# Routing inside the tile loops, weights by expert, and masks turned by the DMA: one change to a two-layer graph and expert network

## The reference, cut to what matters

```python
x = x + gnn0(layernorm(x), adj)    # attention over the neighbours: softmax of h @ h.T where adj > 0
x = x + ffn0(layernorm(x))         # 8 experts, top 2 of each node, hidden 512, silu(x@w1) * (x@w3) @ w2
x = x + gnn1(layernorm(x), adj)    # relu((adj @ x) @ W.T + b)
x = x + ffn1(layernorm(x))         # 8 experts, top 2 of each node, hidden 1024, gelu(x@w1.T + b1) @ w2.T + b2
```

## Time and profile before

| what | us |
|---|---|
| three timed runs | 1803.61, 1805.94, 1807.93 (median 1805.94) |
| the profiled execution, its own time | 1815.38 |
| its span, first to last instruction | 1813.4 |
| mean granted TensorE clock, share of 2.4 GHz | 0.938 |

### The profile page before, as it was taken

How to read it: one execution, slowest core, us unless ns; L and a number is a source line. 1 busy time by engine, 2 the same in 40 slices (tenths; PEclk the granted TensorE clock), 3 DMA queues, 4 the chain that set the end, 5 groups by cost and what they waited for, 6 DMA issues and landing times. The chain is left out here.

```text
span 1813.4 us, 36020 instructions
## 1 busy us (share of the span) xinstructions
PE 1560.3 (86%) x9584; PEld 1297.9 (72%) x9584; DVE 1149.1 (63%) x3860; ACT 638.9 (35%) x1349; POOL 698.7 (39%) x1336
## 2 busy tenths in 40 slices
PE   5899999999999934999999559989618999999994
PEld 5788888888888823888888426555307888888894
DVE  5457777777777766556655356666685666666652
ACT  2323333333333311322233152222205565555562
POOL 0122232233222112767767304333404555455551
PEclk9899999999999966999999869999859999999997
DMA  6233434433333344333323434555341222222223
GB/s 108 86 120 132 149 139 148 149 131 130 130 130 139 102 160 148 53 50 48 50 49 52 101 106 157 195 195 194 110 191 31 41 35 38 38 35 35 38 37 93
DMA packets 85362, 184.70 MB, mean 102 GB/s; under 512 B 19789, under 2 KB 62539, under 8 KB 81291
## 3 DMA queue, kind: packets, MB, share of 16 engines
q1 hardware_dynamic: 57386, 128.02, 21.4%
q0 software_dynamic: 22656, 31.07, 10.8%
q10 hardware_dynamic: 5280, 25.17, 3.5%
HBM read 132.66 MB, written 54.99 MB: 103 GB/s over the span
## 5 line engine op out<-in xcount | busy, mean ns | idle before, releaser
L1056 PE MATMUL bank<-ffn_w_in_parts,ffn_x_t 128*128 128x512 f32 x1416 | 361.7, 404 | 1.7 <-DVE ffn_w_in_parts L1195 1.6
L1080 PE MATMUL bank<-ffn_w_out_parts,ffn_hidden_t 128*128 128x256 f32 x2124 | 285.2, 288 | 19.6 <-DVE ffn_hidden_t L1185 19.6
L1056 PEld LDWEIGHTS bank<-ffn_w_in_parts,ffn_x_t 128*128 128x128 f32 x1416 | 259.4, 191 | 56.0 <-DVE ffn_w_in_parts L1195 5.1
L1080 PEld LDWEIGHTS bank<-ffn_w_out_parts,ffn_hidden_t 128*128 128x128 f32 x2124 | 263.5, 192 | 25.1 <-issue 16.0
L659 PE MATMUL bank<-support,attn_probs_t 128*128 128x512 f32 x650 | 247.8, 414 | 5.7 <-DVE attn_probs_t L533 5.3
L624 PE MATMUL bank<-h_t,attn_h_tile 128*128 128x512 f32 (+1 forms) x1092 | 248.8, 382 | 3.9 <-POOL attn_h_tile L493 3.9
L624 PEld LDWEIGHTS bank<-h_t,attn_h_tile 128*128 128x128 f32 x1092 | 197.0, 189 | 46.1 <-issue 4.1
L521 ACT CAST attn_probs_t<-bank 128x512 fp32r<-128x512 f32 (+1 forms) x182 | 98.7, 557 | 358.5 <-PE bank L633 358.5
L1020 POOL DMA_INDIRECT x<-ffn_y,ffn_dst x118 | 196.5, 1665 | 54.5 <-issue 54.5
L1122 ACT ACTIVATE ffn_silu_or_gelu<-bank,w_b_in 128x128 f32<-128x128 f32 x472 | 134.6, 368 | 156.0 <-PE bank L1067 156.0
L661 PE MATMUL bank<-support,attn_probs_t 128*128 128x256 f32 x676 | 185.5, 281 | 0.0
(11 more groups left out here) (248 smaller groups left out, 2336.5 us busy)
## 6 DMA issues: line engine op xcount, KB each, us to landing
adj_tile<-in_adj SPq DMA_DIRECT2D x25, 1663.5 KB, 7.4
mask<-attn_mask ACTq DMA_DIRECT2D x26, 832.0 KB, 3.4
nbr_mask<-mask SPq DMA_DIRECT2D x26, 832.0 KB, 5.6
w_w_in<-in_w SPq DMA_DIRECT2D x16, 512.0 KB, 10.1
w_w_in<-in_w_t SPq DMA_DIRECT2D x16, 512.0 KB, 4.1
w_w_out<-in_w SPq DMA_DIRECT2D x1, 4096.0 KB, 20.2
x<-attn_x_out SPq DMA_DIRECT2D x26, 128.0 KB, 1.7
xn<-attn_x_normed SPq DMA_DIRECT2D x26, 128.0 KB, 2.3
```

What stands on the lines that cost most here:

```text
L1056: ins = pe.matmul(bank[2 + 2 * slot + b][:, :], XT[:, slot, xp, k, :], WIP[:, wp, k, b * CH:(b + 1) * CH], start=n == 0 and k == 0, stop=n ...
L1080: ins = pe.matmul(bank[7][:, 0:D], HTT[:, hp, k, :], WOP[:, wp, k, :], start=n == 0 and k == 0, stop=n == 2 and k == KH - 1)
```

## The change

The stage `route` is removed, and so are both its calls. Its work is done by tile inside the loops of `attend` and `neighbours`. Each expert has a fixed area of 3328 places in a list in DRAM, so that a pair's place is the expert's base plus a running count. For each tile: PE transposes the normalized rows and multiplies them with the gate weights; DVE picks, ranks and forms the gates; PE counts; POOL scatters (node, gate) of both choices into the list.

```diff
-    def sums(self, dve, t, slot, experts):      # 8 x tensor_tensor_reduce over 256 elements
+    def flip_rows(self, pe, t, slot):           # KD = 2 transposes of XN into PS[slot]
+    def copy_rows(self, act, t, slot):          # PSUM -> XNT, 128x256
+    def multiply_rows(self, pe, t, slot):
+        for k in range(KD):
+            ins = pe.matmul(self.PS[slot][:, 0:E], self.XNT[:, k, :], self.GW[:, k, :], ...)
     def logits(self, dve, t, slot):
+        dve.tensor_tensor(self.L[:, slot, :], self.PS[slot][:, 0:E], self.GB[:], ALU.add)
+    def pick(self, dve, t, slot):
+        link(dve.max(self.M8[:, slot, :], self.L[:, slot, :]))
+        dve.tensor_tensor(self.DIFF[:, slot:slot + 1], ...)
+        link(dve.max_index(self.I8[:, slot, :], self.M8[:, slot, :], self.L[:, slot, :]))
+        link(dve.tensor_copy(self.EF[:, slot, :], self.I8[:, slot, 0:2]))
+        link(dve.tensor_scalar(self.OH[:, slot, :], self.k["IE"][:], self.EF[:, slot, 1:2], None, ALU.is_equal))
+        dve.scalar_tensor_tensor(self.USED[:, slot, :], ...)
+    def count(self, pe, t, slot, rows=P):       # 2 matmuls bf16, 128x128 by 8 columns
+    def rank(self, dve, t, uses, slot):         # 5 instructions over 8 or 2 elements
+    def exp(self, act, t, slot):                # 1 element
+    def gates(self, dve, t, uses, slot):        # 3 instructions over 1 or 2 elements
+    def scatter(self, pool, t, uses, slot):
+        for k in range(2):
+            pool.indirect_dma_start(out=self.pairs, out_offset=...SLI[:, slot, k:k + 1]...,
+                                    in_=self.VALS[:, slot, k, :], in_offset=None)
+    def plan(self, dve):                        # once behind the loop: 12 linked steps on one partition
```

In `attend` PE multiplies the rows of tile t-2 behind chunk 0 and counts behind chunk 2 of the scores; DVE picks and ranks behind the same chunks; the second flip of a tile (g == 1) waits for the ranks of tile t-2 (`ranks_read`); POOL scatters tile t-5 behind the mask. In `neighbours` the order is:

```diff
 SP:   def step(t, ...):
-          sp.wait_ge(flipped, (t - 1) * G)
-          sp.dma_start(NEG[:, slot, :], a["mask"][t, :, :])
+          load_mask(t + 1):  sp.wait_ge(at_ready, t)
+                             sp.dma_start_transpose(MT[:, slot, :, :], a["mask"][t + 1, :, :])
           gate.store(t - 3); store(t - 2), which waits for x_ready; load x(t)
-          w.load_piece(sp, t - 8)
 PE:  +    gate.count(t - 4)
           for g in range(4):
-              flip(...)                         # 26 bf16 transposes in a tile
               multiply(t, slot, g)              # 26 matmuls of 512 columns in a tile
+              g == 0: gate.flip_rows(t - 3)     g == 1: finish(t - 1); gate.multiply_rows(t - 3)
               g == 2: project_out(t - 1)
 DVE:      add(t - 1)
+          gate.rank(t - 4)
-          odd(t, 1); logits(t - 3); odd(t, 3)   # and even(t, 0), even(t, 2) on ACT
+          adjacency(t + 1):  tensor_scalar(AT[:, slot, :, :], MT[:, slot, :, :], 1/BIG, 1.0), 128x3328 bf16 -> f16
+          pick(t - 3); gate.gates(t - 4)
           finish(t - 1)
 POOL:+    gate.scatter(t - 4)
           gate.norm(t)
```

At the start of `neighbours` `adjacency(0)` stands on DVE between `statistics(0)` and `statistics(1)`. The weights of expert 0 are loaded during the stage ahead, on ACT's queue (1.5 MB in `attend`; 2 MB and 1 MB of biases in `neighbours`). The others are loaded by SP inside `experts`, one expert after the other, between the loads of the list:

```diff
+ def load_pairs(t, uses, slot, first, last):
+     if known(t) and t % 4 == 2 and 0 < t // 4 + 1 < E:
+         w.load(sp, t // 4 + 1)                 # waits for the load of the expert before
+     sp.dma_start(PAIRS[:, bass.ds(t * 2, 2)], pairs[bass.ds(row * P, P), :])   # 128 x 8 bytes
```

More of the change, by code:

```diff
@@ L9 @@
 I32 = mybir.dt.int32
+U32 = mybir.dt.uint32
 ALU = mybir.AluOpType
@@ new lines, in copy_rows @@
+    def copy_rows(self, act, t, slot):
+        act.wait_ge(self.xn_flipped, t + 1)
+        if not known(t) or t >= 1:
+            act.wait_ge(self.raw_ready, t)
+        act.copy(self.XNT[:], self.PS[slot][:, 0:D].rearrange("p (k n) -> p k n", k=KD)).then_inc(self.xnt_ready, 1)
+    def multiply_rows(self, pe, t, slot):
+        if known(t) and t == 0:
+            pe.wait_ge(self.w_loaded, 16 if self.gate_b is None else 32)
+        pe.wait_ge(self.xnt_ready, t + 1)
+        for k in range(KD):
+            ins = pe.matmul(self.PS[slot][:, 0:E], self.XNT[:, k, :], self.GW[:, k, :], start=k == 0, stop=k == KD - 1)
+        ins.then_inc(self.raw_ready, 1)
@@ L559, in step, with pick, rank @@
                 def step(t, uses, slot, first, last):
+                    def pick():
+                        gate.logits(dve, t - 2, slot)
+                        gate.pick(dve, t - 2, slot)
+                    def rank():
+                        gate.rank(dve, t - 2, uses - 1, slot)
+                    routed = not known(t) or t >= 2
                     if last:
+                        pick()
+                        rank()
                         rest(t, slot, range(EARLY))
                     else:
[L563 removed]
+                        score(t + 1, 1 - slot, first and slot == 0, lambda: rest(t, slot, range(EARLY)),
+                              {0: pick, 2: rank} if routed else {})
                     for g in range(EARLY, NG):
                         rest(t, slot, [g])
[L566 to L569 removed]
+                        if g == EARLY and routed:
+                            gate.gates(dve, t - 2, uses - 1, slot)
                     dve.wait_ge(exp_done, t + 1)
@@ L605, in _, with scores @@
                 link(dve.tensor_scalar(NATT[:], NATT[:], NSM[:, 3:4], None, ALU.mult))
-                tiles(dve, T, step)
-                gate.sums(dve, T - 1, (T - 1) % 2, range(E))
-                gate.logits(dve, T - 1, (T - 1) % 2)
+                tiles(dve, T, step, head=4)
+                for t in (T - 2, T - 1):
+                    gate.logits(dve, t, t % 2)
+                    gate.pick(dve, t, t % 2)
+                    gate.rank(dve, t, t // 2, t % 2)
+                    gate.gates(dve, t, t // 2, t % 2)
+                gate.plan(dve)
             @block.tensor
             def _(pe):
-                def scores(t, slot, first, midway=None):
+                def scores(t, slot, first, midway=None, behind={}):
                     pe.wait_ge(h_ready, t + 1)
@@ L652, in step @@
                         if EARLY <= g + 1 < NG:
-                            flip(t, slot, g + 1, first)
+                            flip(t, slot, g + 1, first, g + 2 == NG and (not known(t) or t >= 1))
                         pe.wait_ge(lo_ready, t * NG + g + 1)
@@ L1414, in step @@
                         project_out(t, slot)
-                pe.wait_ge(consts, 4)
-                flip(0, 0, 0, 0, True)
+                        gate.count(pe, t - 3, 1 - slot)
+                        for n in (t - 2, t - 1, t):
+                            gate.flip_rows(pe, n, n % 2)
+                            gate.multiply_rows(pe, n, n % 2)
+                            gate.count(pe, n, n % 2, TAIL if n == t else P)
+                pe.wait_ge(consts, 2)
                 pe.wait_ge(w_loaded, 32)
-                tiles(pe, T, step)
+                tiles(pe, T, step, head=4)
             @block.scalar
@@ L1501, in finish, with pick, place @@
                     gate.stats(dve, t, slot)
-                def logits(t, slot):
-                    gate.sums(dve, t, slot, range(E))
+                def pick(t, slot):
                     gate.logits(dve, t, slot)
+                    gate.pick(dve, t, slot)
+                def place(t, uses, slot):
+                    gate.rank(dve, t, uses, slot)
+                    gate.gates(dve, t, uses, slot)
                 def statistics(g):
```

727 lines of the change are left out of this document (358 added, 369 removed).

## The result

Before: median 1804.95 us of 4 runs (1803.61 to 1807.93). After: 1787.69 us of 4 (1786.85 to 1791.93). The ratio is 0.990, with an interval of 0.987 to 0.992: the change gains 1.0%, a small amount that is clear of the noise. The forecast was 1751 us; the time lies within the range of 1725 to 1850, but the gain is 17 us and not 55.

A forecast was written before the change was run, and what follows sets the result against it. PE was taken as the bound (86% busy, full in the attention loop), with some 110 us of routing where it idles. Terms 20 - 34 - 32 + 10 - 33 + 14 = -55 us gave 1751 us from 1805.9; range 1725 to 1850.

The forecast's parts named there:

- The expert stages: +14 us: Both expert stages: later starts and weights loaded beside the loops lengthen them by 14 us together.
- First stage, +11: First expert stage: start +1 us, and scatter landings half as long again over 9 tiles, taken as 10 us.
- Second stage, +3: Second expert stage: start +1 us, and +2 us in the loop, since PE's turn covers the scatter chain.
- +1 each: Start of each expert stage: a list load of about 2 us precedes the first gather, a zero-row wait goes.
- Attention, +20: Attention loop: PE gets 0.76 us more per tile over 26 tiles, paid in full, 20 us.
- Case C: Attention loop: DVE's ranks come late and PE waits about 1 us per tile; 1777 us, chance 0.08.
- First routing, -34: Between last attention matmul and first expert stage: next stage starts at about 667.7 us, not 701.9.
- second -33: Routing behind the neighbour loop: ends at 1322 us, where it was 1355.3; with steps twice as long, gain 20.
- Start of the neighbour stage, +10: Neighbour stage's start: ACT's extra traffic delays the first mask by 6 us, DVE's queued statistics add 4.
- Neighbour loop, -32: Neighbour loop: tile falls from 8.75 to 7.5 us over 25 tiles, 31 us, and 1 for pieces gone.
- case A: Neighbour loop: the turning mask DMA bounds it, with DVE idle; at four times the plain load 1918 us, chance 0.22.
- case B: Neighbour loop: DVE or POOL bounds it at 8.8 us a tile, so it gains nothing; 1783 us, chance 0.18.

The follow-up runs named there:

- the five untouched traces: Traces with unchanged expert stages: the changed kernel, x4, v1, w1 and y1; first expert stage 344.8 to 347.5 us, second 472.0 to 475.3 us.
- x1: Changed kernel, but loads of experts 1 to 7's weights carry 8 columns and every expert uses expert 0's weights; 1756.58 us, ratio 0.971.
- z1: Changed kernel with each expert's weights cut into six DMAs with 1 KB rows, one ahead of each list load; 1774.38 us, ratio 0.979.
- x3: Changed kernel with weights of experts 1 to 7 issued on ACT's queue every three tiles, not on SP's between lists; 1779.2 us, ratio 0.9843.
- x2: Changed kernel with each expert's w_in loaded by four DMAs with 1 KB rows instead of one with 4 KB rows; 1786.76 us, ratio 0.9885.
- w1: Changed kernel without the pair scatter of the last tile in both routings (part of the computation left out); 1784.92 us, ratio 0.986.
- y1: Changed kernel with the first mask's conversion moved behind the fourth group's statistics and third group's lower parts; 1782.33 us, ratio 0.985.
- v1: Changed kernel with each mask loaded by an ordinary DMA instead of the turning one (part of the computation changed); 1783.58 us, ratio 0.9885.
- x4: Changed kernel with the places' conversion to integers, and its wait for the pair scatter, moved behind the mask's conversion; 1785.04 us, ratio 0.987.

## Why the prediction missed

The step that failed is "The expert stages: +14 us". It measured +35 (33 against the mean of the five untouched traces), and x1, which takes the loads of the weights away, is 33 us shorter (17.1 and 16.2). Four things in its working were wrong.
- First stage, +11 forecast, +17.3 measured. "If each landing takes half as long again, that is 1.2 x 9" is near for the landings alone: those of the first seven scatters are 6.6, 3.9, 6.0, 6.9, 7.4, 3.9 and 5.0 us, 12.4 us more than seven quiet ones of 3.9. The seven loads were issued from 689 to 754 and were in flight for 55 us, not 43. What was missing is the gathers that come late in the same bursts, by 4.9 and 4.7 us of standing PE, and a start that is 2.7 us late and not 1. And the price is no share of bandwidth: z1 moves the same bytes in portions, over 86 us instead of 65, and pays 5 us instead of 17.
- Second stage, +3 forecast, +17.4 measured. "PE's turn is longer than that chain, which covers it: +2" took the scatter's chain alone. But on POOL the gather of tile t+2 stands behind the scatter of tile t-2, which waits for the landing of the scatter before it, so a slow scatter and a slow gather come one after the other. PE waited:

```profile
1362.04 0.44 PE L1063 MATMUL bank<-ffn_identity,ffn_x_gathered 128*128 128x128 f32 x2 [2.55 <-DMA ffn_x_gathered<-xn,ffn_tok]
...
1377.67 0.44 PE L1063 MATMUL bank<-ffn_identity,ffn_x_gathered 128*128 128x128 f32 x2 [1.96 <-DMA ffn_x_gathered<-xn,ffn_tok]
...
1402.34 0.69 PE L1063 MATMUL bank<-ffn_identity,ffn_x_gathered 128*128 128x128 f32 x2 [2.73 <-DMA ffn_x_gathered<-xn,ffn_tok]
```

- The start. "+1 each" assumed a quiet first gather. It meets expert 1's weights, issued 1 to 2 us before it, and the first scatter of the second stage comes 4.8 us late (with x1 0.5).
- The clock, which has no term in the sum. From 1 to 2 us before the end of each of the two long waits of the first stage on, PE is granted 1.2 GHz for some 7 us:

```profile
751.00 0.69 PE L1063 MATMUL bank<-ffn_identity,ffn_x_gathered 128*128 128x128 f32 x2 [4.66 <-DMA ffn_x_gathered<-xn,ffn_tok]
```

and the window around and behind this wait, granted clock 0.51 of 2.4 GHz:

```profile
750.00:757.00 7.00, 6.00 (x24) 5.57 (x25) 3.22 (x10) 0.96 (x2) 4.74 (x7) 0.51 0.57 146
```

In the second stage there are seven such stretches of 3.4 us, three of them long after the last load has landed (at 1404), each behind a wait of PE of 1.9 us at a change of expert; there the trace falls back by another 1 us each time. In the kernel before, these waits are 1.6 to 1.7 us and the clock stays at 2.4 GHz there. x1 and x3 have none of these three stretches, x2 has all, z1 two. Scatter by scatter the second stage is 13.6 us behind the one before at the 12th and 17.6 at the 51st. What makes these later waits longer was not tried; x1 also takes one expert's weights throughout, so these 4 us are not shown to be the loads'.

The other terms, by the prediction's own order:
- *Attention, +20: measured +15.5.* Where no tile waited, two stores of a tile's rows were 21.12 us apart before and are 21.91 after, +0.79 against 0.76 forecast. But before, the distances wandered between 21.1 and 23.6, and after nearly all are 21.9 or 22.1. The prediction took PE's full windows to mean that no tile lost time, and they did: about 5 us in all. Case C did not come: PE is busy for 554.9 of 559.3 us.
- *First routing, -34: measured -30.3, second -33: -28.4.* The chains on DVE ran as worked out; both plans ended 14.6 and 23.8 us behind the last matmul or copy. What failed is the time between a plan's end and the next stage: the first sum leaves 2.4 us for it, the second "barrier 1". It is 6.5 and 6.8 us. The small numbers fit a stage whose end waits for DVE (1.6 us in w1). Here it waits for POOL's last scatters and the 4.3 us of POOL's drain behind them; w1 gives 4.9 and 2.7 us for them.
- *Start of the neighbour stage, +10: measured +9.5.* The size was right, and the queue of statistics behind the mask is shown by y1. The mask comes 26.6 us after the stage's start instead of 19.5, forecast +6. With v1's ordinary DMA it is 25.6, so turning is not the reason; that it is ACT's traffic (322 GB/s in the window) is argued, since no run takes that traffic away.
- *Neighbour loop, -32: measured -24.1.* The tile is 7.78 us, not 7.5. PE's own turn is 7.40 us, where 7.45 was forecast, and many tiles reach it. The turning DMA lands in 6.6 us, under the bound of 8.6, so case A is out. The conversion takes 1.03 us, the lower bound of 1.0 to 3.6, so case B is out as well; the 1.9 us of the sum was 0.9 too long. The four elements per cycle of the Trainium skill ("VectorE: DVE Perf Modes") agree with it: 3328 elements in 1.03 us. Its 1309 ns per block, read as the duration of each of 26 in a row, do not: 26 blocks land in 6.6 us. What was late is a wait that the prediction never listed: the rank ends with a wait for the pair scatter of two tiles before, and the conversion of the mask is queued behind it. It named what is queued behind DVE at the mask, and not at the scatter, though both are waits that the change adds. With that wait moved (x4) the loop takes 186.8 us, 31.9 less than before, and the forecast was 32.

So the direction was right, for the reasons given, and the size was wrong by one large and three small terms. Each of the four has to do with an indirect DMA of POOL that was counted by its issue, or by its landing in a quiet chip: behind it came a landing under load (the experts), a drain at the end of a stage (both routings), and a wait that was not listed (the neighbour loop). That the time lies in the stated range is no merit of the sum: the range was kept wide for case A, and the forecast's own 1730 to 1775 was missed. No rival named the cost that came.

## What to carry to other kernels

A load that is "hidden beside the loop" costs what it does to the latency of the loop's serial DMAs, not its bytes over bandwidth: look for the chain that waits for landings, and give the bulk to it in small portions (here 256 KB between the list loads: 23 us in the two stages, 13 to 19 in the whole, for no byte less). Where a change adds a wait on an engine that works its list in order, list all waits that it adds there and put each behind the work that others need first. Look for the end of a stage in the sequencers as well as in the engines: here the landing of POOL's last scatter and POOL's drain behind it cost 3 to 5 us twice. And price a wait of PE with the clock that follows it, 12 of 33 us here.

## What the runs showed of the hardware

- A turning DMA of 832 KB (26 blocks of 128x128 bf16) lands in 6.6 us (median), the ordinary one of the same size in 5.5; but it holds SP for 4.3 us at its issue, and splits into over 3000 packets:

```profile
L1338 SPq DMA_TRANSPOSE nbr_mask_t<-mask x26: 3387/4309/14822, 1043.3 to 1262.9; - x26
L1500 DVE TENSOR_SCALAR nbr_adj_t<-nbr_mask_t x26: 1012/1027/1183, 1060.7 to 1273.0; 128x3328 f16<-128x3328 bf16 x26
```

- DVE turns 3328 bf16 elements per partition into f16 with a multiply and an add in 1.03 us, 0.31 ns each, from SBUF to SBUF.
- An accumulating scatter of 128 KB lands in 3.9 us alone and in up to 8.6 beside bursts of weights in packets of 4 KB; with packets of 1 KB in the same burst ten tiles lose 7.6 us, where they lost 14.4.
- POOL's drain at the end of a block takes 4.3 us behind the tile loops with pair scatters, 2.1 behind the expert loops, and 0.8 behind the tile loops of the kernel before.
- From shortly before the end of waits of PE of 4.7 and 4.9 us on, the granted clock was 1.2 GHz for some 7 us; at changes of expert, behind waits of 1.9 us, it was so three times for 3.4 us.
